# Two lags shortened by one step in a pipelined attention loop, and small transfers moved in the head and before the loop

## The reference, cut to what matters

```python
x = x + quantised_product(layernorm(x), ctx)       # fake-quantised q1 @ q2; ctx is (2, 1024, 1024)
x = x + mixer(layernorm(x))                        # gated state-space layer, in_proj 18560 x 1024, out_proj 1024 x 8192
x = x + lora_experts(layernorm(x))
x = x + point_cloud(coords=ctx, feats=layernorm(x))
x = x + block_sparse_linear(layernorm(x))
x = x + gated_ffn(layernorm(x))

# point_cloud, twice (layer 1 and 2): N = 1024 points, 4 sorted orders, windows of k = 10 neighbours
gf     = concat([center, neigh - center])          # per point, 10 x 512 features, as float16
scores = einsum('bihd,bjhd->bhij', qh, qh) / 8     # 8 heads of 64, 10 x 10 scores per point and head
attn   = softmax(scores)
out    = einsum('bhij,bjhd->bihd', attn, qh)       # "weighted rows"
fused  = out @ W_lin.T + b_lin                     # folded with the convolution: "linear"
h      = max over k of leaky_relu(instance_norm(W_conv @ fused))
```

## Time and profile before

| | us |
|---|---|
| median of 3 runs | 1008.93 (1008.16 to 1011.13) |
| the profiled execution, its own time | 1004.92 |
| span of its profile | 1003.3 |
| PE busy | 955.7 (95%) |
| DVE busy | 737.3 (73%) |
| ACT / POOL busy | 466.8 / 444.4 |

### The profile page before, as it was taken

The page is one execution under the profiler, slowest core; times in us unless marked ns, Lnnn a source line. Parts: engine busy times, 40 slices in busy tenths (PEclk is TensorE's granted clock), DMA queues, the critical chain, the costliest instruction groups (busy, mean ns, idle before and its releaser), DMA issues. The chain is left out here.

```text
span 1003.3 us, 38056 instructions
## 1 busy us (share of the span) xinstructions
PE 955.7 (95%) x15968; PEld 732.2 (73%) x15968; DVE 737.3 (73%) x1930; ACT 466.8 (47%) x764; POOL 444.4 (44%) x408
## 2 busy tenths in 40 slices
PE   2899999999999999999989999999999999999998
PEld 1599878786969697865877776768966666665685
DVE  5788756956666484887968888887789888897410
ACT  4434334141414333212367777774476766765010
POOL 1101211630312112020079999980598888887000
PEclk9999999999999999999999999999999999999999
DMA  8996787967888786565313222232222222221560
GB/s 327 406 405 258 276 308 258 350 265 298 298 299 315 259 323 250 181 253 205 131 53 72 68 68 68 67 73 61 92 64 58 61 55 62 55 61 43 227 278 22
DMA packets 58779, 182.42 MB, mean 182 GB/s; under 512 B 9178, under 2 KB 10954, under 8 KB 58315
## 3 DMA queue, kind: packets, MB, share of 16 engines
q1 hardware_dynamic: 55690, 172.06, 48.7%
q0 software_dynamic: 2432, 8.42, 2.3%
q10 hardware_dynamic: 576, 0.79, 0.3%
HBM read 154.45 MB, written 1.61 MB: 156 GB/s over the span
## 5 line engine op out<-in xcount | busy, mean ns | idle before, releaser
L558 PEld LDWEIGHTS ps<-hT,ring 128*128 128x128 f32 x2304 | 258.1, 192 | 6.7 <-issue 5.7
L558 PE MATMUL ps<-hT,ring 128*128 128x128 f32 x2304 | 260.0, 275 | 0.8 <-ACT xc L705 0.8
L2043 POOL TENSOR_TENSOR X<-sortedT,ring 128x960 f16 (+1 forms) x84 | 156.8, 1867 | 19.7 <-PE ps L1617 19.6
L991 POOL TENSOR_TENSOR y_y<-y_z,sgate 128x512 f32<-128x512 f32 x16 | 20.1, 1273 | 193.0 <-DVE y_z L922 193.0
L591 PE MATMUL ps<-wt,y_n 128*128 128x512 f32 x224 | 99.4, 596 | 1.5 <-DVE xs L914 1.5
L2068 POOL TENSOR_TENSOR PP<-S,PP 128x480 f16<-128x480 f32 x86 | 97.9, 1138 | 5.3 <-ACT PP L1811 5.3
L1636 PE MATMUL ps<-PT,ring 128*64 128x120 f16 x2752 | 96.0, 221 | 4.2 <-issue 1.2
L1636 PEld LDWEIGHTS ps<-PT,ring 128*64 128x64 f16 x2752 | 82.8, 110 | 17.7 <-issue 9.0
L1811 ACT CAST PP<-S 128x480 f16<-128x480 f32 x86 | 66.9, 778 | 61.6 <-POOL S L2061 61.6
L821 DVE SCALAR_TENSOR_TENSOR xc<-xpad,parg,xc 128x128 f32<-128x128 f32 x192 | 59.3, 371 | 42.2 <-ACT xc L705 41.0
L2061 POOL TENSOR_TENSOR S<-S,den 128x480 f32<-128x480 f32 x86 | 86.7, 1009 | 3.9 <-DVE den L1938 3.9
(11 more groups left out here) (330 smaller groups left out, 1549.3 us busy)
## 6 DMA issues: line engine op xcount, KB each, us to landing
ring<-in_w_in SPq DMA_DIRECT2D x36, 2048.0 KB, 8.7
wt<-in_w_out SPq DMA_DIRECT2D x14, 2048.0 KB, 7.8
PT<-P_turned SPq DMA_DIRECT2D x332, 64.0 KB
ring<-in_w SPq DMA_DIRECT2D x8, 1024.0 KB, 12.0
ctx_chunks<-in_ctx SPq DMA_DIRECT2D x4, 1024.0 KB, 9.4
ring<-in_ctx SPq DMA_DIRECT2D x4, 1024.0 KB, 15.8
krow<-keys_scratch POOLq DMA_DIRECT2D x8, 512.0 KB, 7.6
mchunk<-in_mask_t POOLq DMA_DIRECT2D x8, 512.0 KB, 8.7
```

Of the source, the lines that this page charges most:

```text
L558: mm = nc.tensor.matmul(ps[:, bank, j * T:(j + 1) * T], weights[:, j, kc * P:(kc + 1) * P], k.hT[:, kc, :], start=kc == 0, stop=kc == KC - 1)
L2043: ins = gp.tensor_tensor(fcopy(c.X[u][:, 0, 0:1], full(cnt)), fcopy(c.fsT[:, 0, bass.ds(it * STEP, 1)], trio(start, cnt, 1)), fcopy(c.fTr[ ...
```

## The change

Four edits: the two lags and the reduction's lag behind them go down by one; the head's six small loads go from SP's stream to the start of ACT's stream, and the last 1 MB chunk is cut in two halves (9 chunks), with finer waits at its end; all early chunks sit in one buffer; the copies of zeros go from the start of the cloud stage to the experts' stage, behind the load of `wt`, for which the `PT` buffers are allocated earlier.

```diff
@@ stage_quantised_product
-    CHUNKS, KPC = 8, 2
+    KPC = 2
+    chunks = [(b, kc, KPC) for b in range(B) for kc in range(0, KC, KPC)]
+    chunks[-1:] = [(B - 1, KC - KPC, KPC // 2), (B - 1, KC - KPC // 2, KPC // 2)]
+    CHUNKS = len(chunks)
...
             sp.dma_start(k.x[:, :], dr["x"]).then_inc(s_x, 16)
-            load_chunk(0)
-            for i, name in enumerate(("L0_xattn_x1_scale", "L0_xattn_x1_zp", "L0_xattn_x2_scale", "L0_xattn_x2_zp")):
-                sp.dma_start(sc[:, i:i + 1], dr[name].partition_broadcast(P)).then_inc(s_sc, 16)
-            for c in range(1, CHUNKS // 2):
-                load_chunk(c)
-            for b in range(B):
-                sp.dma_start(crow[b * 3 * NT:(b + 1) * 3 * NT, :], ...).then_inc(s_co, 16)
-            for c in range(CHUNKS // 2, CHUNKS):
+            for c in range(CHUNKS):
                 load_chunk(c)
...
-                    sp.wait_ge(s_q2, CHUNKS // 2 + 2 * (j - 1))
+                    sp.wait_ge(s_q2, 6 if j == 2 else CHUNKS)
...
-            v.wait_ge(s_mm, 1)
             v.wait_ge(s_q1, 4)
             for h in range(2):
+                v.wait_ge(s_mm, h + 1)
...
         @block.scalar
+            for i, name in enumerate((... the four scales ...)):
+                act.dma_start(sc[:, i:i + 1], dr[name].partition_broadcast(P)).then_inc(s_sc, 16)
+            for b in range(B):
+                act.dma_start(crow[b * 3 * NT:(b + 1) * 3 * NT, :], ...).then_inc(s_co, 16)
             act.wait_ge(s_const0, 4)
             load_root(nc, k)
...
-                if c == CHUNKS - 1:
+                if c == CHUNKS - 2:
                     row_terms()
@@ stage_lora_experts
             sp.dma_start(k.wt[:, :, :], dr["wt"]).then_inc(k.wt_in, 16)
+            for u in range(2):
+                sp.dma_start(k.PT[u][...], fcopy(k.cloud.X[u][:, 0, :], [[0, 4], [1, N]])).then_inc(k.PT_zeros, 16)
@@
-TURN_LAG, PV_LAG, LINEAR_LAG, REDUCE_LAG = 2, 4, 5, 6
+TURN_LAG, PV_LAG, LINEAR_LAG, REDUCE_LAG = 2, 3, 4, 5
@@ stage_cloud_layer
-        out_bank = lambda it: S_BANK if ending(it) and (STEPS - it) % 2 == 0 else O_BANK
+        out_bank = lambda it: S_BANK if ending(it) and (STEPS - it) % 2 == PV_LAG % 2 else O_BANK
...
-            if layer == 1:
-                for u in range(2):
-                    sp.dma_start(c.PT[u][...], fcopy(c.X[u][:, 0, :], [[0, 4], [1, N]])).then_inc(s_zero, 16)
...
-                pool.wait_ge(s_zero, 32)
+                pool.wait_ge(k.PT_zeros, 32)
```

More of the change, by code:

```diff
@@ L136, in stage_quantised_product @@
 def stage_quantised_product(nc, k, dr):
-    CHUNKS, KPC = 8, 2
-    BUFS = CHUNKS
+    KPC = 2
+    chunks = [(b, kc, KPC) for b in range(B) for kc in range(0, KC, KPC)]
+    chunks[-1:] = [(B - 1, KC - KPC, KPC // 2), (B - 1, KC - KPC // 2, KPC // 2)]
+    CHUNKS = len(chunks)
     with ExitStack() as ctx:
-        early = k.sb("ctx_chunks", [P, BUFS // 2, KPC, D], F32, ctx)
-        cbuf = [early[:, i] for i in range(BUFS // 2)] + [k.ring[:, 8 + KPC * i:8 + KPC * (i + 1), :] for i in range(BUFS // 2)]
+        EARLY_CHUNKS = KC // KPC
+        early = k.sb("ctx_chunks", [P, EARLY_CHUNKS, KPC, D], F32, ctx)
+        cbuf = [early[:, i] for i in range(EARLY_CHUNKS)] + [k.ring[:, 8 + kc:8 + kc + count, :] for b, kc, count in chunks[EARLY_CHUNKS:]]
         q2 = k.sb("q2", [P, B, KC, D], BF16, ctx)
@@ L155, in stage_quantised_product @@
         s_x, s_sc, s_co = k.sem("q_x_in"), k.sem("q_scales_in"), k.sem("q_coords_in")
-        s_ctx = [k.sem(f"q_ctx_in{i}") for i in range(BUFS)]
+        s_ctx = [k.sem(f"q_ctx_in{i}") for i in range(CHUNKS)]
         s_const, s_const0 = k.sem("q_const"), k.sem("q_const0")
@@ L172, in load_chunk @@
             def load_chunk(c):
-                b, kc = c // (CHUNKS // B), c % (CHUNKS // B) * KPC
-                sp.dma_start(cbuf[c], dr["ctx_4096"][b, kc * P:(kc + KPC) * P, :].rearrange("(k p) n -> p k n", p=P)).then_inc(s_ctx[c], 16)
+                b, kc, count = chunks[c]
+                sp.dma_start(cbuf[c], dr["ctx_4096"][b, kc * P:(kc + count) * P, :].rearrange("(k p) n -> p k n", p=P)).then_inc(s_ctx[c], 16)
             sp.dma_start(k.x[:, :], dr["x"]).then_inc(s_x, 16)
-            load_chunk(0)
-            for i, name in enumerate(("L0_xattn_x1_scale", "L0_xattn_x1_zp", "L0_xattn_x2_scale", "L0_xattn_x2_zp")):
-                sp.dma_start(sc[:, i:i + 1], dr[name].partition_broadcast(P)).then_inc(s_sc, 16)
-            for c in range(1, CHUNKS // 2):
-                load_chunk(c)
-            for b in range(B):
-                sp.dma_start(crow[b * 3 * NT:(b + 1) * 3 * NT, :],
-                             dr["ctx_4096"][b, 0:3, :].rearrange("c (t p) -> (c t) p", p=P)).then_inc(s_co, 16)
-            for c in range(CHUNKS // 2, CHUNKS):
+            for c in range(CHUNKS):
                 load_chunk(c)
@@ L231, in _ @@
             for c in range(CHUNKS):
-                b, kc = c // (CHUNKS // B), c % (CHUNKS // B) * KPC
-                buf = cbuf[c % BUFS]
+                b, kc, count = chunks[c]
+                buf = cbuf[c]
                 v.wait_ge(s_aff, c + 1)
@@ L257, in _ @@
         def _(act):
+            for i, name in enumerate(("L0_xattn_x1_scale", "L0_xattn_x1_zp", "L0_xattn_x2_scale", "L0_xattn_x2_zp")):
+                act.dma_start(sc[:, i:i + 1], dr[name].partition_broadcast(P)).then_inc(s_sc, 16)
+            for b in range(B):
+                act.dma_start(crow[b * 3 * NT:(b + 1) * 3 * NT, :],
+                              dr["ctx_4096"][b, 0:3, :].rearrange("c (t p) -> (c t) p", p=P)).then_inc(s_co, 16)
             act.wait_ge(s_const0, 4)
@@ L304, in _ @@
             for c in range(CHUNKS):
-                b, k0 = c // (CHUNKS // B), c % (CHUNKS // B) * KPC
+                b, k0, count = chunks[c]
                 pe.wait_ge(s_q1z, b + 1)
                 pe.wait_ge(s_q2, c + 1)
-                if c == CHUNKS // 2:
+                if b == 1 and k0 == 0:
                     for i in range(B * KC):
@@ L312, in _ @@
                 for to, left in ((csum, lambda kc: onesz[:, b, :]), (acc, lambda kc: q1z[:, b, kc, :])):
-                    for kc in range(k0, k0 + KPC):
+                    for kc in range(k0, k0 + count):
                         first, last = b == 0 and kc == 0, b == B - 1 and kc == KC - 1
@@ L316, in _ @@
                             mm = nc.tensor.matmul(to(h), left(kc), q2[:, b, kc, h * HALF:(h + 1) * HALF], start=first, stop=last)
-                    if c == CHUNKS - 1:
-                        mm.then_inc(s_mm, 1)
+                            if last:
+                                mm.then_inc(s_mm, 1)
             hold_clock(nc, k, 0, 2 * HOLD)
@@ L1042, in _ @@
             sp.dma_start(k.wt[:, :, :], dr["wt"]).then_inc(k.wt_in, 16)
+            for u in range(2):
+                sp.dma_start(k.PT[u][:, :, :, :, :].rearrange("p q s i w -> p q (s i w)"), fcopy(k.cloud.X[u][:, 0, :], [[0, 4], [1, N]])).then_inc(k.PT_zeros, 16)
         @block.tensor
@@ L1385, in __init__ @@
         self.den = [sb(f"den{u}", [P, 2 * SLOTS]) for u in range(2)]
-        self.PT = [sb(f"PT{u}", [P, 4, 2 * SLOTS, 32, 2], F16) for u in range(2)]
+        self.PT = k.PT
         self.PC = [sb(f"P_turned{u}", [P, 2 * SLOTS, 32, 2], F16) for u in range(2)]
@@ L2169, in build @@
         with ExitStack() as sorts:
+            k.PT = [k.sb(f"PT{u}", [P, 4, 2 * SLOTS, 32, 2], F16, sorts) for u in range(2)]
+            k.PT_zeros = k.sem("placed_zeros")
             k.perm_more = k.sb("perm_more", [P, UNITS - IN_RING, HALF], F16, sorts)
```

7 lines of the change are left out of this document (2 added, 5 removed).

## The result

The changed kernel takes 1086.99 us (median of 4 runs) where the kernel before, run beside it, takes 1010.03: a ratio of 1.0755 (95% interval 1.0718 to 1.0792), 76 us slower. A second set of runs gave 1.0748 (1.0714 to 1.0782). The four executions took 1081.6, 1085.1, 1088.9 and 1103.5 us at mean granted clocks of 0.992, 0.990, 0.987 and 0.969, the last one in a slower state, which the ratio leaves out. Forecast were 1077 and the range 1054 to 1098, so range and sign are right; the sum came out near for reasons that partly cancel, and these are the subject of what follows.

A forecast was written before the change was run, and what follows sets the result against it. PE bounds the mixer and both layers' loops; the lowered lags make it wait for DMAs. Lags +77, head -5.5 and zeros -3 give +68.5 on 1008.9, so 1077 us, range 1054 to 1098.

The forecast's parts named there:

- The lags, +77: Both layers' loops: PE's product waits for the PT copies; +38.6 us per loop, +2 per start, -2 per end; bounds +63 to +94.
- the loop over two steps: Closed chain turn, landed DMAs, product, next scores, mx, next turn: 9.81 us per two steps in layer 1, 11.02 in layer 2.
- p = 4.46: Time in us from turn's end until its PT copies landed, read at step 39 of layer 1; bounds 4.1 and 4.90.
- The fourth rival: In the loops, the stall is partly absorbed: SP's issues go faster, p near 3.7, +48, about 1048 us; 8 in 100.
- The clock: Rival for the loops: PE's idle time makes its clock fall for good, +213, 1213 us; 4 in 100.
- The ends: Starts and drains of both layers' loops: first product's wait +2 a layer, one iteration less at the end -2 a layer.
- the head and the zeros bring nothing: Rival: chunks come at their old pace and PE's stop has another cause; 1009 + 77 = 1086 us; 14 in 100.
- The head, -5.5: Kernel's start: DVE's idle time shrinks through earlier crow and scales moved off SP's queue; -5.5 us, bounds -3 and -6.7.
- The -4.5 for the idle time: Head: DVE's 4.5 us idle time before its third chunk goes once crow is issued ahead of most chunks.
- The -1.1 for the scales: Head: scales on their own queue let chunks pass and may land earlier or no earlier; 0 to -2.2, half taken.
- The zeros, -3: Layer 1's gather: moving the zeros' traffic removes PE's 2.24 us stop and the slow clock after it; 0 to -4.1.
- break-even: Loops: the wait from turn's end to landed PT copies at which lower lags neither gain nor lose, about 2.5 us.

The follow-up runs named there:

- experiment 5: Changed kernel with the first of SP's four copies per step cut in two (five issues, same bytes); 1137.22 us, ratio 1.1254 to the kernel before.
- experiment 6: Changed kernel with lags back at 2, 4, 5, 6 and SP's first copy per step cut in two; 1007.98 us, ratio 1.0000 to the kernel before.
- experiment 7: Changed kernel with linear placed ahead of weighted_rows in PE's body, same lags; 1024.62 us, ratio 1.0175 to the kernel before.
- experiment 1: Kernel before with only the three lags lowered to 3, 4, 5; 1094.96 us, ratio 1.0874 to the kernel before.
- experiment 2: Changed kernel with lags back at 2, 4, 5, 6, so head and zeros edits only; 1002.30 us, ratio 0.9936 to the kernel before.
- experiment 3: Kernel before with the head's edit alone, old lags, zeros at the start of the cloud stage; 1005.07 us, ratio 0.9963.
- experiment 4: Kernel before with the zeros' move alone, old lags and old head; 1005.98 us, ratio 0.9965.
- experiment 9: Changed kernel with SP's first copy per step cut in two and ten added unread products a step on PE; 1133.01 us, ratio 1.1210 to the kernel before.
- experiment 11: Changed kernel with old lags, scales on SP behind chunk 0, crow issued by ACT behind the normalisation's root; 1000.41 us, ratio 0.9920 to the kernel before.

## Why the prediction was right, and where it was not

**The lags, +77.** The mechanism held at each link: the wait, its releaser, the loop over two steps, its price per 0.1 us of p (the regular pairs of experiment 5), its absence with lag 4 (experiment 6), and the length of its PE part (experiment 7). In size: +84.7 by the medians, +86.9 by the stretches of the profile, 77 to 88 by experiment 1. Its terms were off in three places.

- *p = 4.46*, "the value read in a running pipeline with no other traffic", is 3.87 to 4.09 in the hardware loops, below even the lower bound of 4.1. Both rows stood in hand-unrolled steps. The bound added the four issues and a landing, 2.4 + 1.7; the last issue's own duration lies within the 2.0 us of its landing. The fourth rival had p right, "near 3.7", though not for its reason: the issues still take 0.59 us each. Scores to `mx` in layer 1 was 0.19 longer (1.15 for 0.96). At the regular pairs the loops would have cost 19 x (9.47 - 7.77) = +32.2 and 19 x (10.59 - 8.99) = +30.4, together 62.6, in place of 77.2. In the unrolled steps p is as long as the rows said or longer (4.4 to 5.8): the steps outside 12 to 36 bring 3.7 more in layer 1, and steps 3, 5 and 7 some 4.7 in layer 2.
- *The clock.* The rival had it fall for good, at +213, or not at all. It fell for single steps, five times in the loops and the drain of the profiled execution, some 8 us in all, four of them (5.8 on the chain of waits) in the loop of layer 2; so without it the changed kernel would be near 1079 (an estimate). The chance of 0.04 was given to the wrong form: an intermediate case was missing. In the loop that the Trainium skill describes in the section that the prediction cites ("TensorE: Matmul & The Clock Gate", section "HAM oscillation — how this bites in real kernels") the clock falls back in each turn; with four copies it did so in few turns here, with five copies in every second pair of layer 2.
- *The ends.* Starts cost 6.1 for 4, ends +3.1 for -4: the drain is no shorter, since it waits for the same copies. In layer 1 the last products still wait up to 1.9 us for `PT`.

These errors cancel: 62.6 + 3.7 (longer p in the unrolled steps of layer 1) + 11.4 (long steps of layer 2, about half p and half clock) = 77.7 for the loops, where 77.2 was forecast. The sum for the loops was near by luck: too large a p in the hardware loops stood in for a longer one in the unrolled steps and for a clock that was not in the sum. And the number alone would have pointed to the wrong story: 1087 is what the rival "the head and the zeros bring nothing" gave (1086), but experiment 2 shows that they bring 6.5 us, and that the lags cost more than +77.

**The head, -5.5.** -3.8 in the profile, -3.7 (-5.4 to -2.1) by experiment 3. The -4.5 for the idle time is right: the wait is gone from the timeline, and DVE's third chunk starts 3.50 us earlier, 4.6 less the 1.1 by which the scales are late. The ninth chunk took 0.2, and the finer waits at the end gave 0.5 (5.01 us for 5.53 behind the last chunk), a term that the sum did not have: -4.6 + 1.1 + 0.2 - 0.5 = -3.8. The -1.1 for the scales had the wrong sign, "they may land earlier or no earlier" left out later. They landed 1.1 later and `x` 1.7 later. The direction of the Trainium skill's rule ("DMA: Bandwidth & Descriptors", section "Issuing engines are not separate DMA queues"), by which they bring nothing, was the better guide; that they delay others is more than the rule says.

**The zeros, -3.** -3.1 in the profile, -3.5 (-4.9 to -2.0) by experiment 4. The size is right, the cause only half shown. The stop of 2.24 us is gone in the changed kernel, but its profile has a fall of the clock of the same cost in the mixer (5 us with a mean clock of 0.66 from 106 us on, as from 483 us on before), so the clock's part of the term was not won there; and stops come without the zeros too. "Layer 2 ... without such a stop" holds for the length only: its gather has stops of 0.63 and 0.35 us at 727 and 730 us before.

**What was to be seen.** PE busy 81% of the loop of layer 1 and 85% of that of layer 2, not below 80%; waits of 0.3 to 1.5 us in nearly each step of layer 1, but in layer 2 in every second one; 4.8 and 5.6 us a step for 4.9 and 5.5. "The prediction is wrong if the product starts less than 4 us behind its turn": it starts 3.87 behind it in most steps of layer 1, and the forecast of a slower kernel held all the same, because break-even was worked out at 2.5.

## What to carry to other kernels

In a pipeline ordered by hand a lag is a budget for one way, here the turn, its copies and their landing; before one takes a step away, that way is to be measured in the hardware loop and in the unrolled steps, each for its own share, and closed into the loop of waits that it would form. A wait placed early in an engine's body holds everything behind it: moving it behind independent work brought back 62 of some 85 us. And idle time of PE has a second price beside its length, since PE may run slower afterwards; the busy time of the same instructions in two profiles gives a first sign of it, and the granted clock in windows of 1 us says how much of it is the clock (8 of 13.3 us here).

## What the runs showed of the hardware

- A copy of 64 KB from one on-chip buffer to another took 1.9 to 2.0 us from the start of its issue to its landing in the hardware loop, and 2.0 to 3.1 in unrolled steps, where single issues took 1.63 to 1.76 us in place of 0.59.
- In the loop of experiment 5, six waits of 2.05 to 2.08 us were each followed by a stretch with a mean clock near 0.64, and six of 1.94 to 1.95 in the same loop by none; in experiment 9 falls came behind waits of 1.46 to 1.49, and in the changed kernel behind one of 1.51 but not behind others of 1.53 and 1.54. One fall took about 1.6 us of PE's work, 1.4 to 1.6 us on the way to the next scores. In the loops of the kernel before the clock stays at 1.00.
- Four broadcasts of a number to 128 partitions at the head of ACT's queue, with two 12 KB loads behind them, delayed the first read of a 512 KB load on SP's queue by 1.7 us; the 12 KB loads alone by 0.7 us; with the 12 KB loads issued only at 6.35 us and the broadcasts on SP's queue again (experiment 11), 0.2 us were left.
- Stops of PE without a releaser in the profile, of up to 2.75 us, came in the gather of layer 1 in eleven of fourteen profiles, at changing places. What makes them was not tried.
